# A two-layer attention kernel: the second layer's output bias moved into the last product, its kept rows moved from VectorE's sum to GpSimd's

## The reference, cut to what matters

```python
def _layer(x, wqkv, qs, ksc, wo, lg, lb, w1, b1, w2, b2):
    ...                                     # local attention, 8 heads
    x = x + o @ wo
    h = shift_token(x)
    h = layernorm(h) * lg + lb
    a, g = jnp.split(h @ w1 + b1, 2, axis=-1)
    x = x + (a * gelu(g)) @ w2 + b2         # 682 hidden channels
    return x

x = x + cross_attention(layernorm(x), ctx)
x = x + layers(layernorm(x))                # two layers, then the outer x once more
```

## Time and profile before

| what | value |
|---|---|
| median of 3 runs | 1527.01 us (1526.02 to 1528.28) |
| the profiled execution's own time | 1526.93 us |
| PE busy | 1441.3 us, 95% of the span |
| DVE busy | 1130.8 us, 74% |
| ACT busy | 938.4 us, 62% |
| POOL busy | 747.1 us, 49% |
| DMA | 58.88 MB, mean 39 GB/s |

### The profile page before, as it was taken

How to read it: one execution, slowest core, us unless ns; L and a number is a source line. 1 busy time by engine, 2 the same in 40 slices (tenths; PEclk the granted TensorE clock), 3 DMA queues, 4 the chain that set the end, 5 groups by cost and what they waited for, 6 DMA issues and landing times.

```text
span 1524.4 us, 33616 instructions
## 1 busy us (share of the span) xinstructions
PE 1441.3 (95%) x11808; PEld 1277.3 (84%) x11808; DVE 1130.8 (74%) x3102; ACT 938.4 (62%) x2670; POOL 747.1 (49%) x570
## 2 busy tenths in 40 slices
PE   4999999867999999999999899999999999999997
PEld 3888888746889889998888788888888888888886
DVE  3766666456888878887878778878888887888864
ACT  2766666435666666666666667666666666666661
POOL 1121121044666666666555555555565555566642
PEclk8999999889999999999999999999999999999998
DMA  6311111200000000000000110010010001011000
GB/s 196 103 57 48 50 53 44 84 29 15 24 24 24 25 25 23 23 23 24 30 31 24 45 41 24 17 47 31 31 32 31 30 30 30 30 34 40 24 24 26
DMA packets 40843, 58.88 MB, mean 39 GB/s; under 512 B 6540, under 2 KB 22448, under 8 KB 40752
## 3 DMA queue, kind: packets, MB, share of 16 engines
q1 hardware_dynamic: 40752, 57.69, 11.7%
HBM read 38.06 MB, written 16.78 MB: 36 GB/s over the span
## 4 chain that ended last, share of the span: by engine, by line
PE 75%; DVE 12%; issue 5%; ACT 4%; POOL 2%; DMA 1%; SPq 1%; DVEq 0%; POOLq 0%; ACTq 0%
PE pb L511 33%; PE pb L788 7%; PE pb L733 6%; PE pb L802 6%; PE pb L764 5%; PE pb L748 4%; PE pb L826 4%; PE pb L572 2%; PE pb L560 2%; PE pb L610 2%; PE pb L614 2%; DVE p_t L1383 2%; DVE r_cos L1350 2%; DVE p_t L1369 1%; DVE n_sq L1336 1%
## 5 line engine op out<-in xcount | busy, mean ns | idle before, releaser
L1559 POOL TENSOR_TENSOR n_inv<-n_cl,half_neg 128x16 f32<-128x16 f32 x64 | 211.4, 3303 | 190.8 <-DVE n_cl L1341 187.3
L1058 ACT ACTIVATE p_t<-p_t,s_nm 128x128 f32<-128x128 f32 (+1 forms) x512 | 227.2, 448 | 19.5 <-DVE s_nm L1369 18.8
L511 PE MATMUL pb<-h_hi,w_hi 128*128 128x256 f32 x704 | 208.8, 297 | 5.3 <-DVE h_lo L1332 3.3
L511 PE MATMUL pb<-h_lo,w_hi 128*128 128x256 f32 x704 | 199.7, 284 | 0.0
L511 PE MATMUL pb<-h_hi,w_lo 128*128 128x256 f32 x704 | 199.7, 284 | 0.0
L1564 POOL TENSOR_TENSOR r_cos<-r_cos,r_sin 128x1024 f32<-128x1024 f32 x64 | 154.7, 2417 | 88.8 <-DVE r_sin L1356 88.8
L1016 ACT ACTIVATE qk_sq<-pb 128x512 f32<-128x512 f32 x128 | 72.5, 592 | 183.6 <-PE pb L511 183.6
L1049 ACT ACTIVATE pt_t<-pb 128x512 f32<-128x512 f32 x192 | 114.5, 597 | 107.0 <-PE pb L748 106.6
L1369 DVE CUSTOM_DVE_ANT_0 p_t<-pb,mask_t 128x128 f32<-128x128 f32 (+1 forms) x512 | 152.0, 353 | 28.5 <-PE pb L733 27.3
L511 PE MATMUL pb<-wqkv_hi,xt_hi 128*128 128x512 f32 x384 | 166.9, 435 | 5.8 <-DVE r_sin L1356 4.9
L1586 POOL TENSOR_TENSOR hg_lo<-hg,hg_hi 128x256 fp32r<-128x256 f32 x192 | 139.6, 748 | 55.4 <-DVE hg_hi L1400 55.4
(11 more groups left out here) (137 smaller groups left out, 4083.1 us busy)
## 6 DMA issues: line engine op xcount, KB each, us to landing
y_state<-x SPq DMA_DIRECT2D x32, 256.0 KB, 2.0
x_cur<-y_state SPq DMA_DIRECT2D x32, 256.0 KB, 2.7
x_res<-y_state SPq DMA_DIRECT2D x32, 256.0 KB, 2.8
x_in<-x SPq DMA_DIRECT2D x16, 256.0 KB, 2.9
x_state<-x SPq DMA_DIRECT2D x16, 256.0 KB, 2.0
x_orig<-x_state SPq DMA_DIRECT2D x16, 256.0 KB, 2.8
out<-x SPq DMA_DIRECT2D x16, 256.0 KB, 2.2
raw_a<-wqkv SPq DMA_DIRECT2D x2, 1536.0 KB, 8.5
```

The source lines that it names most:

```text
L511: mm = pe.matmul(dst, s, m, start=(n == 0 and k == 0), stop=(n == len(pairs) - 1 and k == 2))
L1058: e = nc.scalar.activation(pu, pu, ACT.Exp, bias=s_nm[:, j, k:k + 1], scale=-1.0, accum_out=s_sum[:, j, k:k + 1])
L1559: nc.gpsimd.tensor_tensor(n_inv[:, t], n_cl[:, t], half_neg[:], ALU.pow).then_inc(pool_inv, 1)
```

## The change

- The weights of layer 1's last chunk get two more rows, b2's low and high part, and `hg_hi` holds 1.0 on these two partitions (84 and 127). The third group of 42 moves one partition up, and the DMA that puts the low part of the weights in place copies 43 rows in place of 42. In layer 0 the two rows of the weights are zero.
- `residual_bias` becomes `kept_rows`: in layer 0 it adds b2 as before, in layer 1 it adds `x_orig`, and waits for its load.
- L1412 and its two waits go.
- SP's list has another order: `x_cur`, the wait for x1 of item c, `x_res`, in layer 1 a wait for GpSimd's sum of item c-1 and the load of `x_orig` for item c, then `tail_hi(d)`, `tail_lo(d)`, the wait for `dve_x2` and the store.
- The store has a semaphore for each of its two buffers, and only layer 0's b2 is loaded as a constant (24 DMAs in place of 25).

```diff
-                (b2_t[:, layer], b2[layer].partition_broadcast(P))     # one for each layer
+                (b2_t[:], b2.partition_broadcast(P)),                  # layer 0's
...
-            second, third = slice(TAIL, 2 * TAIL), slice(2 * TAIL, 3 * TAIL)
+            second, third = slice(TAIL, 2 * TAIL), slice(2 * TAIL + 1, 3 * TAIL + 1)
+            rest = slice(TAIL, 2 * TAIL + 1)
...
             def run_l(g, layer=None):
                 a, b, c, d, par = l_roles(g)
+                if has_next(a):
+                    sp.wait_ge(pe_xt, at(a, 1, 1))
+                    sp.dma_start(x_cur[:], one(y_dram, seq_of(plus(a, 1), layer))).then_inc(cur_load, 16)
                 if isinstance(d, int) and d == SEQS:
                     tail_weights(1)
...
+                if c is not None:
+                    sp.wait_ge(dve_x1, at(c, 1, 1))
+                    if b is not None:
+                        sp.dma_start(x_res[:], one(y_dram, seq_of(b, layer))).then_inc(res_load, 16)
+                    if layer_of(c, layer) == LAYERS - 1:
+                        if later(plus(c, -SEQS)):
+                            sp.wait_ge(pool_x1b, at(plus(c, -1), 1, 1))
+                        sp.dma_start(x_orig[:], one(x1_dram, seq_of(c, layer))).then_inc(orig_load, 16)
                 if d is not None:
                     tail_hi(d)
                     tail_lo(d)
-                ...                       (x_cur, x_res, the store and x_orig in the old order)
+                    sp.wait_ge(dve_x2, at(d, 1, 1))
+                    dst = out_rows if layer_of(d, layer) == LAYERS - 1 else y_dram
+                    sp.dma_start(one(dst, seq_of(d, layer)), x2[:, 1 - par]).then_inc(x2_store[1 - par], 16)
...
                 nc.vector.tensor_tensor(x2[:, par].rearrange("p t d -> p (t d)"), pb[:, 7],
                                         x1b[:].rearrange("p t d -> p (t d)"), ALU.add).then_inc(dve_x2, 1)
-                if layer_of(d, layer) == LAYERS - 1:
-                    dve.wait_ge(dve_x2, at(d, 1, 1))
-                    dve.wait_ge(orig_load, at(plus(d, -SEQS), 16, 16))
-                    nc.vector.tensor_tensor(x2[:, par], x2[:, par], x_orig[:], ALU.add).then_inc(dve_out, 1)
...
-            nc.gpsimd.memset(hg_hi[:, FC - 1].bitcast(F32), 0.0).then_inc(zero_made, 1)
+            nc.gpsimd.memset(hg_hi[:, FC - 1].bitcast(F32), 1.0).then_inc(zero_made, 1)
...
+                if layer_of(c, layer) == LAYERS - 1:
+                    pool.wait_ge(orig_load, at(plus(c, -SEQS), 16, 16))
+                    more = x_orig[:].rearrange("p t (c n) -> p t c n", c=KC)
+                else:
+                    more = b2_t[:].rearrange("p (c n) -> p c n", c=KC).unsqueeze(1).broadcast_to([P, NT, KC, P])
+                nc.gpsimd.tensor_tensor(x1b[:].rearrange("p t (c n) -> p t c n", c=KC), x1[:, :, 0:3:2], more,
+                                        ALU.add).then_inc(pool_x1b, 1)
```

More of the change, by code:

```diff
@@ L132, in build @@
         sin_t = sb("sin_t", [P, LAYERS, NT, 2, DH])
[L133 removed]
+        b2_t = sb("b2_t", [P, D])
         b1_t = sb("b1_t", [P, LAYERS, 2, FC])
@@ L251, in build @@
         stats_seen, scores_seen = sem("stats_seen"), sem("scores_seen")
-        cur_load, res_load, orig_load, x2_store = [sem(n) for n in (
-            "cur_load", "res_load", "orig_load", "x2_store")]
+        cur_load, res_load, orig_load = sem("cur_load"), sem("res_load"), sem("orig_load")
+        x2_store = [sem(f"x2_store{u}") for u in range(2)]
         pe_down, dve_down = sem("pe_down"), sem("dve_down")
@@ L442, in _ @@
                 run_x(g)
-            second, third = slice(TAIL, 2 * TAIL), slice(2 * TAIL, 3 * TAIL)
+            second, third = slice(TAIL, 2 * TAIL), slice(2 * TAIL + 1, 3 * TAIL + 1)
+            rest = slice(TAIL, 2 * TAIL + 1)
             def tail_weights(layer):
                 sp.wait_ge(w_lo, WEIGHT["w20" if layer == 0 else "w21"])
-                sp.dma_start(w2_hi[second, FC - 1].bitcast(F32), w2_lo[second, FC - 1].bitcast(F32)).then_inc(tail_w, 16)
+                sp.dma_start(w2_hi[rest, FC - 1].bitcast(F32), w2_lo[rest, FC - 1].bitcast(F32)).then_inc(tail_w, 16)
             def tail_hi(d):
@@ L466, in run_l @@
                 a, b, c, d, par = l_roles(g)
[L467 to L473, removed]
                 if has_next(a):
@@ L476, in run_l @@
                     sp.dma_start(x_cur[:], one(y_dram, seq_of(plus(a, 1), layer))).then_inc(cur_load, 16)
+                if isinstance(d, int) and d == SEQS:
+                    tail_weights(1)
+                if isinstance(g, int) and g == 2:
+                    sp.wait_ge(zero_made, 2)
                 if c is not None:
@@ L480, in run_l @@
                         sp.dma_start(x_res[:], one(y_dram, seq_of(b, layer))).then_inc(res_load, 16)
+                    if layer_of(c, layer) == LAYERS - 1:
+                        if later(plus(c, -SEQS)):
+                            sp.wait_ge(pool_x1b, at(plus(c, -1), 1, 1))
+                        sp.dma_start(x_orig[:], one(x1_dram, seq_of(c, layer))).then_inc(orig_load, 16)
                 if d is not None:
-                    if layer_of(d, layer) == LAYERS - 1:
[L483 to L490, removed]
+                    tail_hi(d)
+                    tail_lo(d)
+                    sp.wait_ge(dve_x2, at(d, 1, 1))
+                    dst = out_rows if layer_of(d, layer) == LAYERS - 1 else y_dram
+                    sp.dma_start(one(dst, seq_of(d, layer)), x2[:, 1 - par]).then_inc(x2_store[1 - par], 16)
             def between(g):
@@ L498, in _ @@
             l_iterations(sp, run_l, between)
-            sp.wait_ge(x2_store, 16 * ITEMS)
+            for u in range(2):
+                sp.wait_ge(x2_store[u], 8 * ITEMS)
         @block.tensor
@@ L1405, in second_residual @@
                 if not isinstance(d, int) or d >= 2:
[L1406 removed]
+                    dve.wait_ge(x2_store[par], of_parity(plus(d, -2)))
                 nc.vector.tensor_tensor(x2[:, par].rearrange("p t d -> p (t d)"), pb[:, 7],
                                         x1b[:].rearrange("p t d -> p (t d)"), ALU.add).then_inc(dve_x2, 1)
[L1409 to L1412 removed]
             def out_lo(b, k):
@@ L1572, in norm_qk, with kept_rows @@
                                         ALU.mult).then_inc(pool_qk, 1)
-            def residual_bias(c, d, layer):
-                ly = layer_of(c, layer)
+            def kept_rows(c, d, layer):
                 pool.wait_ge(dve_x1, at(c, 1, 1))
@@ L1605, in run_l @@
                 if c is not None:
-                    residual_bias(c, d, layer)
+                    kept_rows(c, d, layer)
                     gate_lo(c, 0)
@@ L1637 @@
     w2 = rows_padded(L0_ffn_w2, FC * P)
-    for copy in (1, 2):
-        w2[:, HID + (copy - 1) * TAIL:HID + copy * TAIL] = w2[:, HID - TAIL:HID]
+    tail = w2[:, HID - TAIL:HID]
+    w2[:, HID:HID + TAIL] = tail
+    w2[:, HID + TAIL + 1:HID + 2 * TAIL + 1] = tail
+    for row in (HID + TAIL, HID + 2 * TAIL + 1):
+        w2[LAYERS - 1, row] = np.asarray(L0_ffn_b2)[LAYERS - 1]
     by_channel = lambda v: np.ascontiguousarray(np.asarray(v).reshape(LAYERS, KC, P).transpose(0, 2, 1))
```

8 lines of the change are left out of this document (2 added, 6 removed).

## The result

The changed kernel takes 1511.34 us (median of 4 runs, 1510.82 to 1513.41) against 1527.64 (1526.02 to 1529.03) for the one before: a ratio of 0.9896, 95% interval 0.9879 to 0.9913. The forecast was 1515.3, the range ended at 1513.5: right in direction, too small in size, and the median lies 2.2 us outside. Two more sets of the same kernel gave 1512.93 and 1512.54. So the first set was the lowest of three, and part of its distance to the forecast is luck. Over all sets the kernel before has a mean of 1526.6 (56 runs) and the changed one of 1512.4 (14 runs), 14.2 us less, where 11.6 were forecast.

What follows compares the result with a forecast made beforehand. TensorE, busy 95% of the span, bounds the kernel; in layer 1 the extra sum pushes VectorE's list past TensorE's. Savings 6.6 + 3.5 + 0.3 + 0.7 + 0.5 = 11.6 us from 1526.9 give 1515.3; range 1513.5 to 1520.5.

Steps and rivals of the forecast that it cites:

- The loop and the unrolled iterations: Layer 1: without the extra sum, eight loop iterations lose 0.82 us each (6.6) and five unrolled ones 0.69 each (3.5).
- Rival 1: Layer 1: only TensorE's idle time, 5.3 us, comes back; with the ends 6.8 us, giving 1520.1; chance 0.12.
- rival 4: Layer 1's longer iteration is due to x_orig's load, which stays; only the ends are saved, some 1525.4; chance 0.04.
- GpSimd's sum and SP's order: GpSimd's sum with a full second operand, and copies of the last chunk queued behind two loads: nothing for either.
- rival 2: Layer 1: GpSimd's sum grows by 0.26 us and delays VectorE's copies, 13 times, 3.4 us, 1518.7; chance 0.05.
- rival 3: Iterations 3 to 31: the last chunk's copies come late, making it slower; one microsecond late gives 1544; chance 0.04.
- Iteration 32: Drain: the extra sum's removal shortens the chain ahead of TensorE's `hidden`; between 0.2 and 0.7 us, 0.3 taken.
- the last sum: Iteration 34, end of the drain: only the store waits for the extra sum, so its removal saves 0.7 us.
- The constant: Start: one constant fewer for SP to issue makes everything behind it 0.5 us earlier; bounds nothing and 1.0.
- Iteration 33: Drain: the extra sum lies under ScalarE's scaling of h, which ends last, so its removal saves nothing.
- the better bounds of the ends: Start and drain: all ends at their better bound give 1.0 us less, 1514 as the forecast's own lower end.

Runs made afterwards that it cites:

- put-back run: Changed kernel with an unused VectorE sum of the removed one's size put back in iterations 32 and 33 only: 1512.43 us, ratio 0.9911.
- the longer layer 1 alone: Changed kernel with the same-sized unused VectorE sum put back in iterations 19 to 31 and not in 32 and 33: 1523.48 us, ratio 0.9982.

## Why the forecast came out too small

**The loop and the unrolled iterations: right.** Forecast 8 x 0.82 and 5 x 0.69, 10.1 us. Iterations 20 to 31 gave 8.8 and the turn of the layers, which holds iteration 19, 0.8 by the means of the profiles with and without the sum there (191.7 and 190.8, six and eight profiles); where the forecast's terms stand for the same 12 periods they make 9.3 (8 x 0.82 + 4 x 0.69). A loop period fell by 0.75 us and not 0.82, to 36.02 and not to 35.95; what the last 0.07 us are was not looked into. Putting the sum back gave the old 440.5 us back. Rival 1 (5.3 us here) is refuted, and so is rival 4 (nothing here).

**GpSimd's sum and SP's order: nothing each in the loops, as forecast.** The sum takes 1348 ns where it took 1347, so rival 2 is refuted. TensorE's last chunk never waited for its copies, and with the old order the loops took the same: rival 3 is refuted. In iteration 33 that chunk began at 1487.56 without a wait, `tail_lo` having been issued at 1484.39. How thin this place is, which the working had said, shows in the one wait of 0.53 us above. What it had not: that the early `x_orig` costs the drain 0.9 us by GpSimd's sum.

**Iteration 32: 0.44 for 0.3, and the last sum 0.7: right.** The put-back run gave 31.41 us with the clock full, so the 0.44 is the sum's.

**The constant: too small.** The step took the issues alone, 0.5 us. Over the profiles, the last constant is issued some 0.6 us earlier with 24 than with 25, the first keys' product comes 0.8 earlier (22.98 and 23.81, standard error 0.3), and the first mark is reached after 388.5 us (mean of eight profiles) instead of 389.8 (seven): 1.3 us, standard error 0.6. That the bytes of the broadcast count too, which stood as the upper bound "1.0", fits these numbers and isn't shown by them.

**Iteration 33: the step that failed.** It said: "In iteration 33 the sum lies under ScalarE's scaling of h, which ends last: nothing." From the mark of iteration 32 to the end 3.53 us were saved in the profiled pair, where 0.7 were forecast. Two things were missing: a hold of 0.45 us, and a clock that can cost up to 2.7.

One is on the path always. The extra sum did end ahead of h; but it ran beside GpSimd's x1b sum and lengthened that from 1.26 to 1.71 us, and this reached into the copy of h and held it, 1.34 us instead of 0.89. That is 0.45 us on the path: 1.34 to 1.37 in all five profiles with the extra sum in iteration 33, 0.89 to 0.93 in all without it, but for the one with SP's old order and `x_orig` late (0.44). The earlier trace rows had shown such a hold, and I weighed it at the loop and forgot it here. The Trainium skill, "SBUF — State Buffer", section "SBUF: two separate sides", calls the pair of ports that the two engines share an exclusive lock; the trace agrees: with 1.71 us as with 1.26 for GpSimd's sum, the copy ends 0.29 us behind its end (1501.92 and 1501.63 before, 1490.38 and 1490.09 after).

The other is the clock, and it hangs on more than this iteration. The step took the 60 products as fixed, where the pair of profiles has 9.89 and 7.44 us. With the wait filled in both kernels, the means are 1524.1 and 1513.0: 11.1 us, where 11.6 were forecast. With the wait as it is they are 1526.6 and 1512.4: 14.2. The difference of 3.1 us (1.6 either way by the scatter of the runs) is an upper guess at what the fall of the clock in iteration 33 adds: a single fall costs 1.4 to 2.7 us in the profiles, so it cannot add more than that. Neither pays it in every execution: the products took 9.9 us in two of three profiles of the kernel before and 10.0 in one of three of the changed kernel. The mean granted clock of the timed runs is 0.9803 in the kernel before and 0.9839 in the changed one; among the runs of the kernel before, a line through time and clock gives 0.66 us for each 0.001, so this difference goes with 2.4. But it is a mean over the whole span and doesn't say where: filling the wait brought the kernel before to 0.9825 only.

What it isn't was tested. It isn't the sum in that iteration alone: without it the products still took 10.13 us, and with it the changed kernel still had a median of 1512.4 (mean 1513.1). It isn't the length of the wait, 2.84 or 3.30 us: each has both outcomes. That it goes with the time at which the wait comes is a guess that two runs point to and don't prove: 2.8 us of products three iterations ahead cost the changed kernel 2.9 us beyond themselves, with a mean clock of 0.981, and the longer layer 1 alone brought the clock to 0.981 too. What decides the fall stays open.

The rest can be added up from what was measured by stretches: 9.6 us for the loop and the unrolled iterations, 0.44 for iteration 32, 0.45 for the hold, 0.7 for the last sum, 1.3 for the start, 0.2 around the span, 12.7 us in all. Of the 14.2 that leaves 1.5 us, with a doubt of nearly as much, for the clock of the end: the part of the gain that is the place in time, or chance, and not the change's work.

**The range: too narrow.** Its lower end added the better bounds of the ends, 1.0 us and a rest. One term had no bound below its value at all: the 9.89 us of products, which the granted clock of that stretch would have priced at up to 2.45 (9.89 less 7.44). And single runs of either kernel scatter with a deviation of 1.4 us, so a median of 4 has some 0.7 of its own. The other two sets of the changed kernel, 1512.5 and 1512.9, lie below the range too.

## What to carry to other kernels

The difference between two periods of one loop, measured in its two layers, forecast the loop's gain within a tenth; the sum of the waits would have been half of it. At the ends, lay the granted clock beside each stretch where TensorE comes out of a wait of some microseconds, and give the range what the stretch would save at full clock, even if the change doesn't touch it: the same kernel has such a stretch at either clock from one execution to the next. Where such a wait stays, unused products in it are cheap and took this kernel from 1512.4 to 1508.1 us (means of 14 and 8 runs); nearly all of that came from the long waits at the start and at the turn of the layers.

## What the runs showed of the hardware

- The granted clock of TensorE fell from 1.00 to 0.50 in the same wait of the same kernel in some executions and not in others, in the wait or up to 2 us behind it, with waits of 2.39 to 3.30 us; 60 products then took between 8.80 and 10.13 us instead of 7.44. With the wait filled by 20 or 24 products they took 7.44 in each of the four profiles.
- Three instructions can hold each other in a row: a VectorE sum of 128x512 with both operands on chip stretched GpSimd's sum from 1.26 to 1.71 us, and that stretched a 128x512 copy on VectorE from 0.44 (nothing beside it) over 0.89 to 1.34.
- On GpSimd a 128x512 sum took 1348 ns with two full operands and 1347 with a broadcast one.
- One broadcast constant of 25 ahead of the first keys' product cost 0.8 us there (standard error 0.3), where its issue takes 0.43 to 0.48.
